# Cross-attention of a decoder layer: context also loaded transposed, log-exp-Newton inverses, stack rows interleaved

## The reference

```python
def _L0_xattn_ref(q, k, v, gamma):      # q = layernorm(x), k = v = ctx_2048, all (16, 256, 512)
    qh = q.reshape(B, h, dq, Lq)        # h = 8 heads of dq = 32 rows; Lq = Lk = 512
    ...
    qk = jnp.einsum('bhdq,bhdl->bhql', qh, kh) * scale
    sm = jax.nn.softmax(qk, axis=-1)
    ret = jnp.einsum('bhql,bhdl->bhdq', sm, vh)
    return gamma * ret.reshape(B, Dv, Lq)
x = x + _L0_xattn_ref(_layernorm(x, axis=-1), ctx_2048, ctx_2048, L0_xattn_gamma)
```

## Time and profile before

| | |
|---|---|
| median of 3 runs | 2759.67 us (2757.46 to 2761.4) |
| profiled execution, its time | 2760.93 us |
| profiled execution, its span | 2759.2 us |
| cross-attention, from its first load to its last statistics | 1959.3 to 2560.7 us of the span |
| mean granted clock of TensorE | 0.978 |

### The profile page before, as it was taken

How to read it: one execution, slowest core, us unless ns; L and a number is a source line. 1 busy time by engine, 2 the same in 40 slices (tenths; PEclk the granted TensorE clock), 3 DMA queues, 4 the chain that set the end, 5 groups by cost and what they waited for, 6 DMA issues and landing times. The chain is left out here.

```text
span 2759.2 us, 38367 instructions
## 1 busy us (share of the span) xinstructions
PE 2626.3 (95%) x13448; PEld 1973.6 (72%) x13448; DVE 1755.7 (64%) x3663; ACT 985.4 (36%) x2469; POOL 861.7 (31%) x698
## 2 busy tenths in 40 slices
PE   6999999999999999999999999999599999999794
PEld 5888888888888888888887888888344444444683
DVE  5777776665655665655665665666467776665557
ACT  2332223222222323222232222222267777776220
POOL 3211112221211322111132221111268887777000
PEclk9999999999999999999999999999699999999797
DMA  3123223222211323211122311110567676662003
GB/s 115 62 92 108 107 77 126 73 82 102 77 61 62 100 69 117 82 62 62 62 100 93 114 62 62 62 62 31 176 180 186 186 185 181 183 181 62 20 1 122
DMA packets 162476, 272.28 MB, mean 99 GB/s; under 512 B 11504, under 2 KB 78064, under 8 KB 162288
## 3 DMA queue, kind: packets, MB, share of 16 engines
q1 hardware_dynamic: 162288, 269.82, 31.6%
HBM read 176.98 MB, written 92.27 MB: 98 GB/s over the span
## 5 line engine op out<-in xcount | busy, mean ns | idle before, releaser
L346 PE MATMUL pj<-xnt,whi 128*128 128x512 f32 x2048 | 705.8, 406 | 5.1 <-DVE xnt L580 5.1
L439 ACT ACTIVATE pr<-sc,nmx 128x128 f32<-128x128 f32 (+1 forms) x512 | 211.1, 417 | 929.0 <-DVE nmx L525 929.0
L291 POOL TENSOR_TENSOR qt<-rot,swp 128x512 f32<-128x512 f32 x128 | 166.0, 1297 | 1107.2 <-DVE swp L505 1107.2
L346 PEld LDWEIGHTS pj<-xnt,whi 128*128 128x128 f32 x2048 | 387.0, 189 | 97.9 <-DVE xnt L580 5.8
L979 DVE TENSOR_REDUCE xnmx<-xsc 128x1 f32<-128x512 f32 x512 | 336.4, 684 | 163.2 <-PE xsc L799 160.2
L346 PE MATMUL pj<-xnt,wlo 128*128 128x512 f32 x1024 | 399.7, 390 | 0.0
L769 POOL TENSOR_TENSOR xprt<-xprt 128x512 f32<-128x512 f32 x256 | 320.2, 1280 | 119.8 <-PE xob L819 91.0
L343 PE MATMUL pj<-whi,xnt 128*128 128x512 f32 x1024 | 352.9, 406 | 4.0 <-issue 4.0
L921 ACT ACTIVATE xprt<-xst 128x512 f32<-128x512 f32 x512 | 290.6, 596 | 112.3 <-PE xst L808 108.8
L503 DVE TENSOR_TENSOR rot<-pj,trig 128x512 f32<-128x512 f32 x256 | 176.6, 690 | 212.5 <-PE pj L346 212.5
L799 PE MATMUL xsc<-kst,qst 96*128 96x512 f32 x512 | 235.4, 464 | 34.2 <-DMA kst<-sk_scratch 31.7
(11 more groups left out here) (190 smaller groups left out, 4341.8 us busy)
## 6 DMA issues: line engine op xcount, KB each, us to landing
xnt<-xt_scratch SPq DMA_DIRECT2D x48, 1024.0 KB, 7.5
x_scratch<-xio SPq DMA_DIRECT2D x64, 512.0 KB, 3.6
xio<-x_scratch SPq DMA_DIRECT2D x48, 512.0 KB, 4.1
qst<-sq_scratch SPq DMA_DIRECT2D x96, 256.0 KB, 5.0
kst<-sk_scratch SPq DMA_DIRECT2D x96, 256.0 KB, 5.7
raw<-in_w_all_dram SPq DMA_DIRECT2D x64, 256.0 KB, 4.7
xt_scratch<-xnt SPq DMA_DIRECT2D x16, 1024.0 KB, 8.8
sq_scratch<-qp SPq DMA_DIRECT2D x32, 512.0 KB, 8.1
```

The source lines that it names most:

```text
L291: nc.gpsimd.tensor_tensor(qk["QK".index(kind)][h][:, :, :].rearrange("p b n -> p (b n)"), rot[r % 2][:, :], swp[r % 2][:, :], ALU.add).the ...
L346: last = nc.tensor.matmul(bank[:, :], wpart[:, w, i * HD:(i + 1) * HD], moving, start=(k == 0), stop=(k == 3 * CB - 1))
L439: nc.scalar.activation(pr[:, a % 4, lo:hi], SC[a % 2][:, lo:hi], ACT.Exp, bias=nmx[:, a % 4, t:t + 1], accum_out=rsum[:, a % 4, t:t + 1]). ...
```

## The change

The context comes a second time as an input, laid out transposed on the host (`ctx_t`), and `load_values` loads it straight to `vt`, which has three buffers. `values` and `v_evac` go.

The sums stay in PSUM, in two banks (`SU`), repeated over the 32 rows of a head as before. ScalarE takes their logarithm (`log_of_sums`) and the exponential of its negative (`inverse_of_sums`); VectorE improves it by one Newton step of two operations in place (`newton`, `newton_end`), and `output` multiplies with the bank. `sums_by_query`, `reciprocal`, `repeat`, `inverses` and `sums_evac` go. Gamma moves into `output_evac`.

`qp` and `kp` get two buffers, `prt` has six instead of five. One set of activation tables, which has both functions, is loaded ahead; the inverse square roots of the layernorm come from VectorE alone, in 17 small steps. The stack rows are interleaved: row 3r+c of a stack is part c of row r, where it was row 32c+r. `weigh(s-1)` moves to the middle of step s, and `sums` to the end of steps 0 and 2.

```diff
             def load_context(m):
                 if m >= 4:
-                    sp.wait_ge(s_vt, m - 3)
                     sp.wait_ge(s_klo, m - 3)
                 sp.dma_start(cin[:, m % 4, :], cv[m]).then_inc(s_ci[m % 4], 16)
 
+            def load_values(m):
+                if m >= 3:
+                    sp.wait_ge(s_pv, CB * (m - 2))
+                sp.dma_start(vt[:, m % 3, :, :], ctx_t[m]).then_inc(s_vt[m % 3], 16)
...
                 for c in range(PARTS):
-                    rows = slice(XD * c, XD * (c + 1))
+                    rows = slice(c, KS, PARTS)
                     sp.dma_start(qst[m % STACKS][rows, :, :].bitcast(F32), qv[c // 2]).then_inc(s_st[m % STACKS], 16)
                     sp.dma_start(kst[m % STACKS][rows, :, :].bitcast(F32), kv[c % 2]).then_inc(s_st[m % STACKS], 16)
...
-                    if i == 1:
-                        middle(s // CB, s % CB)
-                if 0 <= s - 1 < STEPS:
-                    weigh(s - 1)
+                    if i == 1 and s % CB == 2 and tile(s // CB + 1):
+                        max_transposes(s // CB + 1)
+                    if i == 1 and 0 <= s - 1 < STEPS:
+                        weigh(s - 1)
+                if s % CB in (0, 2) and tile(s // CB - 1):
+                    sums(s // CB - 1, s % CB // 2)
...
             def q_round(m):
                 act.wait_ge(s_qn, m + 1)
-                act.wait_ge(s_qw, 16 * m)
-                nc.scalar.activation(qp[:, 0, :], xn[:, :], ACT.Copy).then_inc(s_qhi, 1)
+                if m >= 2:
+                    act.wait_ge(s_qw, 16 * (m - 1))
+                nc.scalar.activation(qp[m % 2][:, 0, :], xn[:, :], ACT.Copy).then_inc(s_qhi, 1)
...
+            def log_of_sums(n):
                 act.wait_ge(s_su, 2 * n + 2)
-                act.wait_ge(s_sq, n)
-                nc.scalar.activation(ssb[:, :], SU[:, :], ACT.Copy).then_inc(s_se, 1)
+                act.wait_ge(s_new, 2 * n)
+                nc.scalar.activation(rin[:, :], SU[n % 2][:, :], ACT.Ln).then_inc(s_log, 1)
+
+            def inverse_of_sums(n):
+                act.wait_ge(s_log, n + 1)
+                nc.scalar.activation(rin[:, :], rin[:, :], ACT.Exp, scale=-1.0).then_inc(s_inv, 1)
...
-            WORK = {(0, 0): ((k_round, 3),), (0, 1): ((repeat, -2),), (0, 2): ((v_evac, 0),), (1, 0): ((output_evac, -1),),
-                    (1, 1): ((normed, 4),), (1, 3): ((q_round, 4),), (2, 2): ((max_round, 1),), (2, 3): ((sums_evac, -1),)}
+            WORK = {(0, 0): ((k_round, 3),), (0, 2): ((output_evac, -1),), (1, 1): ((normed, 4),), (1, 3): ((q_round, 4),),
+                    (2, 2): ((max_round, 1),), (3, 0): ((log_of_sums, -1),), (3, 2): ((inverse_of_sums, -1),)}
...
+            def newton(n):
+                dve.wait_ge(s_inv, n + 1)
+                nc.vector.scalar_tensor_tensor(SU[n % 2][:, :], SU[n % 2][:, :], -1.0, rin[:, :],
+                                               ALU.mult, ALU.mult).then_inc(s_new, 1)
+
+            def newton_end(n):
+                dve.wait_ge(s_new, 2 * n + 1)
+                nc.vector.scalar_tensor_tensor(SU[n % 2][:, :], SU[n % 2][:, :], 2.0, rin[:, :],
+                                               ALU.add, ALU.mult).then_inc(s_new, 1)
...
-            WORK = {(0, 1): ((statistics, -3),), (0, 2): ((mean_and_variance, -3),), (2, 0): ((output, -2),),
-                    (2, 2): ((max_rest, 1),), (3, 3): ((one_over_sums, -1),)}
+            WORK = {(0, 0): ((statistics, -3),), (0, 1): ((newton, -2),), (0, 2): ((mean_and_variance, -3),),
+                    (0, 3): ((newton_end, -2),), (1, 1): ((output, -2),), (2, 2): ((max_rest, 1),)}
```

More of the change, by code:

```diff
@@ L818, in weigh @@
                     rows = slice(XD * h, XD * (h + 1))
-                    last = nc.tensor.matmul(OB[rows, :], vt[:, n % 2, c, rows], prt[s % RING][:, h, :],
+                    last = nc.tensor.matmul(OB[rows, :], vt[:, n % 3, c, rows], prt[s % RING][:, h, :],
                                             start=(c == 0), stop=(c == CB - 1))
@@ L824, in sums @@
                 pe.wait_ge(s_add, XPT * (2 * n + k + 1))
-                if k == 0:
-                    pe.wait_ge(s_se, n)
+                if k == 0 and n >= 2:
+                    pe.wait_ge(s_on, n - 1)
                 for h in range(XPT):
                     rows = slice(XD * h, XD * (h + 1))
-                    last = nc.tensor.matmul(SU[rows, :], ones[:, :], prt[(CB * n + 2 * k) % RING][:, h, :],
+                    last = nc.tensor.matmul(SU[n % 2][rows, :], ones[:, :], prt[(CB * n + 2 * k) % RING][:, h, :],
                                             start=(k == 0), stop=(k == 1))
                 last.then_inc(s_su, 1)
-            def values(n):
-                pe.wait_ge(s_ci[n % 4], 16 * (n // 4 + 1))
-                if n >= 2:
-                    pe.wait_ge(s_ri, n - 1)
-                for c in range(CB):
-                    last = nc.tensor.transpose(VB[:, c * P:(c + 1) * P], cin[:, n % 4, c * P:(c + 1) * P], ident[:, :])
-                last.then_inc(s_vt, 1)
             def max_transposes(n):
@@ L844, in max_transposes @@
                 nc.tensor.transpose(MX[0:XPT * CB, 0:P], nmx[:, n % 2, :], ident[:, :]).then_inc(s_mt, 1)
-            def sums_by_query(n):
-                pe.wait_ge(s_se, n + 1)
-                pe.wait_ge(s_vte, min(n + 2, TILES))
-                pe.wait_ge(s_on, n)
-                for q in range(CB):
-                    last = nc.tensor.matmul(VB[:, q * XPT:(q + 1) * XPT], ssb[:, q * P:(q + 1) * P], ident[:, 0:P:XD],
-                                            start=True, stop=True)
-                last.then_inc(s_sq, 1)
-            def inverses(n):
-                pe.wait_ge(s_rr, n + 1)
-                pe.wait_ge(s_vte, min(n + 3, TILES))
-                for q in range(CB):
-                    last = nc.tensor.transpose(VB[:, q * P:(q + 1) * P], rrep[:, q, :], ident[:, :])
-                last.then_inc(s_rt, 1)
-            def middle(n, c):
-                if c == 0:
-                    if tile(n - 1):
-                        sums(n - 1, 0)
-                    if tile(n):
-                        values(n)
-                if c == 1 and tile(n - 2):
-                    inverses(n - 2)
-                if c == 2:
-                    if tile(n - 1):
-                        sums(n - 1, 1)
-                    if tile(n + 1):
-                        max_transposes(n + 1)
-                if c == 3 and tile(n - 1):
-                    sums_by_query(n - 1)
             pe.wait_ge(s_ones, STACKS + 1)
```

111 lines of the change are left out of this document (46 added, 65 removed).

## The result

The changed kernel takes 2739.07 us (median of 4 runs, 2736.91 to 2744.02), beside 2759.77 for the kernel before on the same chip (4 runs). The ratio is 0.993, 95% interval 0.9915 to 0.9945: 20.7 us faster. The forecast was 41.9 us faster. So the direction held and the time lies in the range, but half of the expected gain is missing. In the profiled executions the span went from 2759.2 to 2742.3. The one of the changed kernel took 2744.02, 5 above its median, so of the 41.9 forecast 25 are missing in these traces and 21 between the medians.

The account below looks back on a forecast made before the run. TensorE's own issue was taken as the bound: tile 14.7 + 0.54 + 0.43 + 0.17, taken as 15.9 against 17.16 us. Over 30.5 tiles 38.4, plus 1.9 + 1 + 0.6, gives 2760.9 - 41.9 = 2719; range 2700 to 2757.

Parts of the forecast that it names:

- TensorE's tile of 15.9: Steady cross-attention: one tile was to take 15.9 us instead of 17.16, set by TensorE's issue and ring waits.
- The floor's "1.6": TensorE's work per tile without waits, 16.4 us before: values, inverses, sums by query and maxima counted as 1.6.
- the walk: One new-order tile followed through its four steps, placing matmuls, maxima and exponentials: total 15.8 us.
- the walk's 0.54 + 0.17: Step 0: TensorE leaves 0.54 us late through VectorE's ring; its second transposed score waits 0.17 for ScalarE's last exponential.
- The rate lies between the two rows: Interleaved stack reads: between 216 and 406 GB/s, taken as 300, so 5.2 us of moving, in time by 0.9.
- the 1.8 fixed: Stack reads: fixed part of the time from issue to use, 1.8 us beside the moving.
- The prediction's own limit: Stack reads: they stay hidden behind TensorE's work up to 6.1 us of moving.
- The first rival: Stack reads get no faster and bind the tile: 17.3 us per tile, 2764 us in total; chance 0.14.
- some 0.7 us of short waits: Kernel before, per tile: TensorE's short waits on the score rings and stack reads, above its 16.4 floor.
- I estimate 1965.2, 1.7 later: Stage start: layernorm's scales ready 1.7 us later, from 17 small VectorE steps, 12 of them at 0.23.
- 2.3 back: Stage start: the first stack reads were to give back 2.3 us.
- Writes of VectorE to PSUM, the output's chain and the end: Newton operations 0.69 us latency; chain after last sums 2.9 instead of 4.8; last one and a half tiles gain 1.

Follow-up runs that it names:

- stacks4: Changed kernel with a fourth stack buffer, exponentials' ring cut from 6 to 5, `vt` from 3 to 2, `kp` from 2 to 1; 2723.86 us.
- experiment 8: stacks4 without VectorE's two Newton operations, the inverses written straight to the bank of the sums; 2726.11 us, one run.
- before_woven: Kernel before the change with only the stack rows interleaved; 2743.85 us, ratio 0.9939.
- ones_late: Changed kernel with GpSimd's fills with ones moved behind its first work on queries and keys; 2737.72 us, ratio 0.9915.
- rows_apart: Changed kernel with the stack rows' interleaving undone, all else as changed; 2777.58 us, ratio 1.0055.

## Why the prediction was right and wrong

- **TensorE's tile of 15.9 was right to 0.15.** stacks4 measures 15.95 in the mean once the reads are out of the way, 16.0 to 16.1 from tile to tile, and the changed kernel's own best tiles take 16.0. Two terms were small by 0.1 to 0.2. The floor's "1.6" for values, inverses, sums by query and maxima is the first three alone (0.41 + 0.35 + 0.81); the maxima's transposes take 0.2 more (2205.04 to 2205.24 in stacks4), and the walk leaves them out too. And the junction at step 0 costs 0.8, against the walk's 0.54 + 0.17. Its parts were wrong as well: VectorE's load with the Newton operations was not the reason (experiment 8), the maxima's round trip costs 0.4, and ScalarE's late exponential costs 0.4 and not 0.17. The one at step 2 costs 0.4, as the walk had it. The "15.9, since hand-offs vary" covered most of that.
- **The step that failed** is "The rate lies between the two rows; near the middle, 300 GB/s, gives 5.2 us and landing at 0.26 + 1.8 + 5.2 = 7.3, in time by 0.9". The mechanism was right, interleaving does make the reads faster, but the term was mis-sized. The scores used the reads 8.2 to 9.4 after issue, which with the 1.8 fixed is 6.4 to 7.6 us of moving, for 1.57 MB at 207 to 246 GB/s. The prediction's own limit was 6.1. So TensorE waited for the reads 0.76 us per tile in the mean, where they should have been early by 0.9. I had chosen the middle between two rows that were of different things, 32 partitions and 128. The rate is only one part of it. At the 264 that the best stretch shows for the reads, 1.57 MB take an estimated 6.0 us and would just have been in time. The "1.8" was carried over from reads of another pattern and was too small as well: in the tile above the same 6.0 leave 2.4 of the 8.35. The bytes start later (0.12 MB after 2.1 us against 0.34 MB). An issue with partitions at step three takes 0.60 us instead of 0.43, and the next row stands 0.645 behind instead of 0.475; that the late start comes of this was not tested. And most reads come later than that tile's, by up to 2 us, for which the sum had no term.
- **The cost of being late was larger than the wait**, since after some of the waits the granted clock falls: after the longest, of 2.3 us, and after one of 1.33, where it is 0.50 from 2329.5 to 2332.5. After one of 1.42 it stayed at 1.00 (2194.5 to 2197.5). The two tiles around the longest wait lost 3.7 us to a wait of 2.3. The prediction had no term for it.
- **The first rival's formula was right for its own case.** With the rows apart an undisturbed tile takes 17.26 against its 17.3; the total was 14 us above it by the clock. That is how near the change was to being a loss: all but one line of it, alone, is 17 us slower than before.
- **"some 0.7 us of short waits" before** was near: with the floor put right it is 0.5 to 0.6, and before_woven shows that about 0.5 goes with faster reads. That ScalarE's wait for the stores of `qp` costs TensorE little was taken without a run, and before_woven leaves it open: that wait shrank from 34.7 to 12.3 us together with the tile.
- **The start was mis-sized**: "I estimate 1965.2, 1.7 later" became 4.5 later. Twelve steps at 0.23 were priced from a row that no fill touched. The first three of the 17, of a form that GpSimd's fills hold up, took 1.43, 1.82 and 1.82. The kernel before shows it too (rows above): its first such step took 1.43 and a later one 0.66, while a step with two tensors as inputs took 0.19 beside the same fills. I had not looked at these rows. The Trainium skill, page "SBUF — State Buffer", section "Who interferes with whom", has VectorE and GpSimd take turns at a port that they share for such operations. ones_late agrees: with the fills elsewhere the same steps take 0.18.
- **The "2.3 back" at the start** came out in size: 4.5 were lost on the scales and 2.3 by the first transposes, so 2.2 came back. It isn't shown that the first reads gave it. rows_apart, without faster reads, has 1.2 of it (30.7 us from scales to transposes, before 31.8, changed 29.6), and before_woven, with them, has none. This stays open.
- **Writes of VectorE to PSUM, the output's chain and the end** were right: 0.689 per operation, 2.76 against 2.9, 3.2 us gained against 2.9.
- **`vt` and GpSimd at no cost** held. Even with `vt` in two buffers and a tile of 15.95 no wait for it shows, and GpSimd fits into the same tile.

## What to carry to other kernels

A transfer that is just in time is a term to be bounded, not to be put at the middle: work out the rate at which it becomes late (here 1.57 MB in 6.1 us, 257 GB/s), put bounds on the fixed part too when the pattern of the transfer changes, and if the nearest rows lie on both sides, weigh "late" as the likely case, or give it one more buffer, which here was worth 15 us between the medians. When a change shortens the loop, every hidden transfer has to be held against the shorter loop: the same reads that were in time in a tile of 16.7 were late in one of 15.9. Where TensorE waits at a ring, more work of its own costs little up to the length of the wait; here 1.3 us per tile were hidden. And look at the rows around a chain of tiny operations before pricing it by one of them, since an engine that fills memory beside them can make each eight to ten times as long.

## What the runs showed of the hardware

- **The pattern of partitions changes a read's rate.** Three reads per stack to 32 neighbouring partitions each moved 199 GB/s, one read to 96 neighbours 223, three to every third of 96 up to 277 with a store's bytes, alone at most an estimated 264. Stores and loads over 128 partitions moved 406. The Trainium skill, page "SBUF — State Buffer", section "Can I just issue two DMAs to hit both halves?", says that only a transfer over all 128 partitions reaches all ports. The trace agrees in that none of the three comes near 406; that the interleaved ones gain so much over the others is in no row of that page.
- **An issue with partitions at a step costs more**: 0.60 us against 0.43, and 0.33 for the first of a group at no step.
- **A long wait of TensorE is paid twice.** After 2.3 us of waiting, the clock granted over the next 3 us was 0.54, and a weighing took 1.93 instead of 1.07. Of the shorter waits some were followed by it (1.33 us) and some not (1.42).
- **Fills by GpSimd hold up VectorE's small steps**: three fills, 5.51 us in all, made three steps of 0.18 us (`tensor_scalar` on 128x32) last 1.43, 1.82 and 1.82. In the kernel before a `tensor_tensor` of that size took 0.19 beside such a fill.
- **Two junctions hide 1.3 us of TensorE's work.** Where four pairs of score matmuls ran unparted through two banks, idle matmuls worth 1.54 us per tile made the tile only 0.25 longer; at parted places, matmuls worth 0.88 made it 0.88 longer.
